# A state-space input stage fully unrolled over three chunks in flight, with the convolution accumulated in PSUM, and the y of the scan taken one state later

## The chip, the core and the metric

The kernel runs on one core of one Trainium2 chip. The metric is the time of one execution on the device in microseconds, as the median of several runs. The engines are TensorE (PE; its weight loads are PEld), VectorE (DVE), ScalarE (ACT), GpSimd (POOL) and SyncE (SP), which issues the DMAs.

## The reference

Four layers follow each other on a (4, 1024, 256) input: a Mamba layer, a top-2 mixture of experts, an attention, and a mixture in which the experts choose their tokens. The change lies in the first one only, whose mathematics is this (channels d_inner = 512, states 16, 4 taps):

```python
xz = hidden_states @ in_proj_w
x, z = jnp.split(xz, 2, axis=-1)
...
for k in range(D_CONV):
    acc = acc + conv_w[:, k] * xpad[:, k:k + seqlen, :]
x = jax.nn.silu(acc + conv_b)
x_dbl = x @ x_proj_w
dt_low, Bm, Cm = jnp.split(x_dbl, [DT_RANK, DT_RANK + D_STATE], axis=-1)
dt = jax.nn.softplus(dt_low @ dt_proj_w + dt_bias)
...
    dA = jnp.exp(dt_t[:, :, None] * A)
    dBu = dt_t[:, :, None] * B_t[:, None, :] * u_t[:, :, None]
    h = dA * h + dBu
    y_t = jnp.einsum('bdn,bn->bd', h, C_t)
...
y = jnp.swapaxes(y, 0, 1) + D_param * x
y = y * jax.nn.silu(z)
return y @ out_proj_w
```

## The kernel before

The layer runs as three blocks with a barrier between them: layernorm with a transpose, the input stage `mamba_front`, and the scan `mamba_scan`. All arithmetic here is float32; only the split B and C rows are bfloat16.

**Input stage.** The 4096 tokens are cut into 8 chunks of CH = 512. A chunk has MT = 4 blocks of 128 channels for x and 4 for z. For each of the 8 blocks TensorE multiplies with `w_in` into one of three PSUM banks (0, 1, 3; line 322). ScalarE copies the x blocks into `xpad` (369), VectorE runs the 4-tap convolution from `xpad` into `conv` in SBUF: one tensor_scalar (426) and three scalar_tensor_tensor (430) per block, with two blocks interleaved so that each instruction waits for the one before the last. ScalarE applies Silu to z (378) and to `conv` (381, giving `xc`, the u of the scan). TensorE multiplies `xc` with `w_x` (333) to 96 rows: 64 rows `dt_low`, which ScalarE copies (363), and 32 rows B and C, which VectorE copies (440) and splits into three bfloat16 parts (442 to 456). TensorE multiplies `dt_low` with `w_dt` (345) into the four PSUM banks 4 to 7.

The softplus is max(v, 0) + log(1 + e^-|v|), where the logarithm gets a correction for the rounding of its argument: VectorE takes the positive part `relu` (410), ScalarE |v| (388) and the exponential e (391), VectorE w = 1 + e (446), ScalarE the logarithm `lw` (394), VectorE the correction (w - 1) - e (450), GpSimd adds `relu` to `lw` (474), VectorE subtracts the correction (463), which gives `dt`, and GpSimd multiplies dt by `xc` (479), which gives `du`. SyncE writes z, x, B and C, dt and du of the chunk to DRAM, 1 MB each but for the 64 KB of B and C.

Step q does the head of chunk q (in_proj, convolution, Silu) and the tail of chunk q - 1 (x_proj, dt_proj, softplus). Every engine walks the steps in its own written order; the steps 2 to 7 are three rounds of a hardware loop of two steps each. Buffers `xc` and `zs` are double; ScalarE waits ahead of its z blocks until GpSimd has finished `du` of two chunks before, which reads the `xc` that is to be overwritten: `act.wait_ge(soft_pool, SP * (q - 1))`.

**Scan.** A unit is one state s of one channel block m of one batch b, over the whole sequence of 1024: 256 units. For 12 of 16 states TensorE spreads a row of B over the partitions (624), VectorE multiplies it with `du` in PSUM (705); for the four states 3, 7, 11 and 15 GpSimd makes the product (775). ScalarE makes dA (687), VectorE runs the recurrence (717), GpSimd multiplies with C (788), and TensorE sums the 16 states of a group into banks 4 and 5 with an identity (634), three units late (`LAG = 3`). The finished sum of a group is read by VectorE in the next group: `take_y` (724) adds D * x, `gate_y` (734) multiplies with silu(z), and out_proj (646) follows a batch later, with its additions to the residual (739).

```python
if s == FIN and not first:
    take_y(*before)
scan(b, m, s, first)
```

`FIN` is LAG - 1 = 2 here: VectorE reads y ahead of the recurrence of state 2. TensorE's sum for state 0 of the new group waits for `y_read`, since it overwrites the banks.

## Time and profile before

| What | us |
|---|---|
| Median of 3 runs | 3065.36 (3064.15 to 3067.4) |
| The profiled execution | 3070.39, of it span 3068.4 |
| Layernorm and transpose | 0 to 36.2 |
| Input stage | 36.2 to 343.5 |
| Scan with its out_proj | 343.5 to 1235 |
| The three other layers | 1235 to 3068.4 |

In rows by stage the engines stand in the order PE, PEld, DVE, ACT, POOL. The profile gives, for each engine, busy time, single instructions with their start and length, and the idle time ahead of an instruction with the instruction that ended it. The granted clock of TensorE (PEclk) is 1.00 at 2.4 GHz and 0.50 at 1.2 GHz. A float32 matmul appears as two passes, each with its weight load. The four stages follow each other behind barriers, so a stage that ends earlier moves all that follows.

### The profile page before, as it was taken

How to read it: one execution, taken by the hardware profiler on the slowest of the kernel's cores; microseconds unless marked ns; L12 is line 12 of the kernel's file. 1: busy time of each engine (PE TensorE's matmuls, PEld its weight loads, DVE VectorE, ACT ScalarE, POOL GpSimd, SP SyncE). 2: the span in 40 equal slices, each digit the busy share in tenths (PEclk: the TensorE clock that was granted, in tenths of full speed). 3: DMA queues.
4: the chain of work that ended last, by engine and by line, in shares of the span. 5: the costliest groups of instructions: out<-in, count | busy, mean ns of one | idle time of the engine just before them, and what ended most of it. 6: DMA issues, size and time to landing. Idle time of an engine off the chain costs nothing. (4 is left out here: it accounts for less than half of the span.)

```text
span 3068.4 us, 36222 instructions
## 1 busy us (share of the span) xinstructions
PE 2399.6 (78%) x10411; PEld 1261.6 (41%) x10413; DVE 1995.2 (65%) x2898; ACT 1028.3 (34%) x1511; POOL 1265.6 (41%) x696
## 2 busy tenths in 40 slices
PE   6676377777777877389994669999999733999998
PEld 3222132333333333256773313444444321666666
DVE  6888899999999998643333787868686265121110
ACT  3554333333333332212222605646465420211111
POOL 0334688888888887046651320000000001233332
PEclk9877688988988999689996859999999855999999
DMA  3333612313214110644433331202020032232322
GB/s 109 132 119 111 223 52 96 124 42 115 90 41 147 59 41 14 215 105 65 65 60 77 103 39 29 42 18 40 18 39 2 4 110 77 59 72 62 82 60 30
DMA packets 141562, 228.91 MB, mean 75 GB/s; under 512 B 25536, under 2 KB 89600, under 8 KB 141120
## 3 DMA queue, kind: packets, MB, share of 16 engines
q1 hardware_dynamic: 115312, 191.23, 20.0%
q0 software_dynamic: 26112, 35.96, 7.3%
q8 instruction: 72, 1.18, 0.2%
q14 instruction: 66, 0.54, 0.1%
HBM read 149.81 MB, written 77.34 MB: 74 GB/s over the span
## 5 line engine op out<-in xcount | busy, mean ns | idle before, releaser
L788 POOL TENSOR_TENSOR scan_hC<-scan_h,scan_c_all 128x1024 f32<-128x1024 f32 x256 | 612.2, 2404 | 108.3 <-DVE scan_h L717 106.5
L634 PE MATMUL banks<-scan_hC,all_ident 128*128 128x512 f32 x1024 | 534.1, 656 | 1.7 <-POOL scan_hC L788 1.7
L717 DVE TENSOR_TENSOR_SCAN scan_h<-scan_dA,banks 128x1024 f32<-128x1024 f32 x192 | 438.9, 2286 | 17.6 <-ACT scan_dA L687 1.6
L1760 ACT ACTIVATE attn_pt<-banks 128x256 f32<-128x256 f32 (+7 forms) x512 | 314.3, 651 | 333.8 <-PE banks L1688 329.6
L687 ACT ACTIVATE scan_dA<-scan_dt,mamba_a_neg 128x1024 f32<-128x1024 f32 x192 | 220.7, 1150 | 416.1 <-DVE scan_h L717 412.6
L1781 DVE TENSOR_REDUCE attn_m_lo<-banks 128x1 f32<-128x512 f32 (+3 forms) x512 | 288.1, 587 | 79.3 <-PE banks L1636 53.6
L624 PE MATMUL banks<-mamba_bc_parts,scan_pick 96*128 (+1 forms) x384 | 137.0, 444 | 242.6 <-DVE scan_h L717 206.9
L634 PEld LDWEIGHTS banks<-scan_hC,all_ident 128*128 128x128 f32 x1024 | 217.2, 212 | 206.6 <-issue 180.0
L1633 PE MATMUL banks<-attn_K,attn_Q 96*128 96x512 bf16 (+3 forms) x768 | 248.2, 357 | 44.9 <-DVE attn_mask L1773 27.4
L2250 DVE TENSOR_TENSOR ffn_y<-banks,ffn_gates 128x512 f32<-128x512 f32 x32 | 22.1, 692 | 358.6 <-PE banks L2149 351.8
L705 DVE TENSOR_TENSOR banks<-scan_du,banks 128x1024 f32<-128x1024 f32 x192 | 232.0, 1208 | 3.2 <-DMA scan_du<-scratch_du 3.2
L1686 PE MATMUL banks<-attn_Q,attn_K 99*128 99x512 bf16 (+3 forms) x768 | 209.3, 335 | 25.6 <-ACT attn_pt L1760 12.0
L2149 PE MATMUL banks<-ffn_w,ffn_hT 128*128 128x256 f32 x1024 | 228.6, 380 | 0.0
L2133 PE MATMUL banks<-ffn_xgT,ffn_w 128*128 128x512 f32 x512 | 228.5, 599 | 0.0
L2086 POOL DMA_INDIRECT out<-ffn_y,ffn_ids x64 | 101.0, 1578 | 296.7 <-DVE ffn_y L2250 287.0
L1616 POOL COPY attn_V<-attn_v_all 128x256 f32 x12 | 4.8, 402 | 505.2 <-PE banks L1705 505.2
L2149 PEld LDWEIGHTS banks<-ffn_w,ffn_hT 128*128 128x128 f32 x1024 | 191.9, 190 | 28.5 <-issue 4.3
L624 PEld LDWEIGHTS banks<-mamba_bc_parts,scan_pick 96*128 96x128 bf16 x384 | 31.6, 106 | 401.3 <-DVE scan_h L717 306.3
L2075 POOL DMA_INDIRECT ffn_xg<-scratch_xn_rows,ffn_ids x64 | 62.8, 981 | 307.1 <-DVE ffn_ids L2235 284.3
L1705 PE MATMUL banks<-attn_pt,attn_V 128*32 128x512 f32 (+3 forms) x1536 | 162.9, 499 | 1.7 <-issue 0.7
L775 POOL TENSOR_TENSOR scan_dBu<-scan_du,scan_b_all 128x1024 f32<-128x1024 f32 x64 | 150.9, 2358 | 11.6 <-DMA scan_b_all<-scratch_bc 11.6
L1633 PEld LDWEIGHTS banks<-attn_K,attn_Q 96*128 96x128 bf16 x768 | 76.6, 101 | 190.4 <-DVE attn_m_lo L1781 65.4
(267 smaller groups left out, 3814.8 us busy)
## 6 DMA issues: line engine op xcount, KB each, us to landing
scan_c_all<-scratch_bc SPq DMA_DIRECT2D x64, 512.0 KB, 4.8
ffn_w<-in_e_w SPq DMA_DIRECT2D x16, 1024.0 KB
attn_Q<-scratch_q SPq DMA_DIRECT2D x96, 128.0 KB
scratch_z<-front_zs SPq DMA_DIRECT2D x8, 1024.0 KB
scratch_x<-front_xc SPq DMA_DIRECT2D x8, 1024.0 KB
scratch_dt<-front_dt SPq DMA_DIRECT2D x8, 1024.0 KB
scratch_du<-front_du SPq DMA_DIRECT2D x8, 1024.0 KB
scan_dt<-scratch_dt SPq DMA_DIRECT2D x16, 512.0 KB, 6.2
```

The source lines that it names most:

```text
L624: mm = pe.matmul(PS[:, (s % 2) * HALVES + i, :], pick[:, s, :], bc_parts[:, bass.ds(b * SEQ + i * BANK, BANK)], start=True, stop=True)
L634: mm = pe.matmul(PS[:, YB + i, :], ident[:, :], hC[:, s % NHC, i * BANK:(i + 1) * BANK], start=s == 0, stop=s == NST - 1, skip_group_check ...
L687: act.activation(to, dt[:, m % 2, :], ACT.Exp, scale=a_neg[:, m, s:s + 1]).then_inc(dA_done, 1)
L705: dve.tensor_tensor(pair_of(s), du[:, m % 2, :], pair_of(s), ALU.mult).then_inc(dve_bu, 1)
L717: dve.tensor_tensor_scan(h[:, s % 2, :], decay, drive, 0.0, ALU.mult, ALU.add).then_inc(scanned, 1)
L788: pool.tensor_tensor(hC[:, s % NHC, :], h[:, s % 2, :], c_all[:, s, :], ALU.mult).then_inc(hC_done, 1)
L1633: mm = pe.matmul(PS[:, bank, at:at + width], Q[0:KR, mkv, j, tile * P:(tile + 1) * P], K[0:KR, mkv, k0:k0 + width], start=True, stop=not d ...
L1686: mm = pe.matmul(PS[:, b0 + i, 0:wd], K[:, kv, kb * P:(kb + 1) * P], Q[:, kv, j, kb * P + at:kb * P + at + wd], start=True, stop=i > 0, sk ...
L1760: act.activation(pt[:, kb % 2, j, 0:width], PS[:, SB_ + (j % 2) * 2:SB_ + (j % 2) * 2 + 2, :].rearrange("p a n -> p (a n)")[:, 0:width], A ...
L1781: op = dve.tensor_reduce(dst, PS[:, bank, at:at + width], AX, ALU.max)
L2133: mm = pe.matmul(PS[:, HB + (hp % 2) * 2 + i, :], w1[:, s, k, (2 * hp + i) * P:(2 * hp + i + 1) * P], xgT[:, pr, k, :], start=k == 0, stop ...
L2149: mm = pe.matmul(PS[:, YB + z, hf * DM:(hf + 1) * DM], hT[:, pr, c, j * P:(j + 1) * P], w2[:, s, c, :], start=c == 0, stop=c == HC - 1, sk ...
```

## The change

`mamba_front` is written anew, and in `mamba_scan` one number changes.

- Three chunks are in flight in place of two. Step q (of 10, all unrolled, no loop) does the head of chunk q, the projections and |v| of chunk q - 1 (`mid`), and the exponential, logarithm and the rest of the softplus of chunk q - 2 (`tail`). `xc` has four buffers.
- The convolution of a block accumulates in PSUM bank 3 and only its last tap writes `conv` in SBUF. With one bank for it the four blocks run one after the other, each instruction waiting for the one just before it.
- The positive part is not kept: `relu` and e are added in the PSUM bank of v, `less` = (w - 1) - (relu + e) is made from it by VectorE, and GpSimd's `lw - less` is dt. The second pass of VectorE over dt (463) is gone.
- The rows of `w_x` are reordered, so that B and C come first, and ScalarE copies all 96 rows at once into `xd`; a row of ones in `xd` and a row of `w_dt` carry dt_bias. Three memsets of 512 columns prepare `xd` and `w_dt`, and TensorE and ScalarE wait for them (`made`) ahead of their first instruction.
- The x, x_proj and z results rotate through the banks 0 to 2; each waits until the result three places before it was read.
- `FIN = LAG`: y is taken ahead of state 3, behind the recurrence of state 2.

In the diff below, removed lines that the code above shows already are left out.

```diff
-    w_dt = n.sb("w_dt", [RANK, DI])
+    w_dt = n.sb("w_dt", [XD + 1, DI])
...
+                               (w_x[:, :, 0:NBC], g["w_x"][:, RANK:XD].rearrange("(m p) n -> p m n", p=P)),
+                               (w_x[:, :, NBC:XD], g["w_x"][:, 0:RANK].rearrange("(m p) n -> p m n", p=P)),
+                               (w_dt[NBC:XD, :], g["w_dt"]),
+                               (w_dt[XD:XD + 1, :], g["dt_bias"].rearrange("(o d) -> o d", o=1)),
...
+        XS = 4
+        xc = n.sb("xc", [P, XS, MT, CH])
+        xd = n.sb("xd", [XD + 1, 2, CH])
+        less = n.sb("less", [P, MT, CH])
...
+        NIN, CBANK, DTBANK = 3, 3, 4
...
+        STEPS = range(NCH + 2)
+        PLACES = []
+        for q in range(NCH + 1):
+            PLACES += [("x", q, m) for m in range(MT) if head(q)]
+            PLACES += [("xd", q - 1, 0)] if mid(q) else []
+            PLACES += [("z", q, m) for m in range(MT) if head(q)]
+        def bank_of(kind, q, m):
+            return PLACES.index((kind, q, m)) % NIN
...
+            for q in STEPS:
+                if tail(q):
+                    c = q - 2
+                    sp.wait_ge(dt_done, MT * (c + 1))
+                    sp.dma_start(chunk_of("dt", c), lw[:, :, :]).then_inc(out_dt, 16)
+                    sp.wait_ge(du_done, MT * (c + 1))
+                    sp.dma_start(chunk_of("du", c), du[:, :, :]).then_inc(out_du, 16)
+                if mid(q):
+                    c = q - 1
+                    sp.wait_ge(xd_copied, c + 1)
+                    sp.dma_start(dram["bc"][:, c * CH:(c + 1) * CH], xd[0:NBC, c % 2, :]).then_inc(out_bc[c % 2], 16)
+                if head(q):
+                    sp.wait_ge(silu_x, MT * (q + 1))
+                    sp.dma_start(chunk_of("x", q), xc[:, q % XS, :, :]).then_inc(out_x[q % XS], 16)
+                    sp.dma_start(chunk_of("z", q), zs[:, q % 2, :, :]).then_inc(out_z[q % 2], 16)
...
+            def dt_proj(c):
+                pe.wait_ge(xd_copied, c + 1)
+                for m in range(MT):
+                    if c:
+                        pe.wait_ge(less_done, MT * (c - 1) + m + 1)
+                    pe.matmul(PS[:, DTBANK + m, :], w_dt[:, m * P:(m + 1) * P], xd[:, c % 2, :],
+                              start=True, stop=True).then_inc(dt_psum, 1)
+            for q in STEPS:
+                if head(q):
                     for m in range(MT):
+                        in_proj("x", q, m)
+                if mid(q):
+                    x_proj(q - 1)
+                if head(q):
+                    for m in range(2):
+                        in_proj("z", q, m)
+                if mid(q):
+                    dt_proj(q - 1)
+                if head(q):
+                    for m in range(2, MT):
+                        in_proj("z", q, m)
...
+            for q in STEPS:
+                if tail(q):
+                    c = q - 2
+                    act.wait_ge(dt_abs, MT * (c + 1))
+                    act.activation(u[:, :, :], u[:, :, :], ACT.Exp, scale=-1.0).then_inc(exp_done, 1)
+                if head(q):
+                    for m in range(2):
+                        copy_x(q, m)
+                if tail(q):
+                    c = q - 2
+                    act.wait_ge(w_done, c + 1)
                     for m in range(MT):
+                        act.activation(lw[:, m, :], w[:, m, :], ACT.Ln).then_inc(ln_done, 1)
+                if head(q):
+                    for m in range(2, MT):
+                        copy_x(q, m)
+                if mid(q):
+                    c = q - 1
+                    act.wait_ge(xd_psum, c + 1)
...
+                    act.activation(xd[0:XD, c % 2, :], PS[0:XD, bank_of("xd", c, 0), :], ACT.Copy).then_inc(xd_copied, 1)
+                if head(q):
+                    for m in range(2):
+                        silu_z(q, m)
+                    for m in range(2):
+                        silu_conv(q, m)
+                if mid(q):
+                    c = q - 1
                     for m in range(MT):
+                        act.wait_ge(dt_psum, MT * c + m + 1)
+                        act.activation(u[:, m, :], PS[:, DTBANK + m, :], ACT.Abs).then_inc(dt_abs, 1)
+                if head(q):
+                    for m in range(2, MT):
+                        silu_z(q, m)
+                    for m in range(2, MT):
+                        silu_conv(q, m)
...
-            dve.memset(xpad[:, :, 0:NTAP - 1], 0.0).then_inc(pad_zero, 1)
+            dve.memset(xpad[:, :, 0:NTAP - 1], 0.0).then_inc(made, 1)
+            for s in range(2):
+                dve.memset(xd[XD:XD + 1, s, :], 1.0).then_inc(made, 1)
+            dve.memset(w_dt[0:NBC, :], 0.0).then_inc(made, 1)
...
+            def convolve(q, m):
+                h = q % HB
+                acc = PS[:, CBANK, :]
+                for tap in range(NTAP):
+                    src = xpad[:, m, h * CH + tap:h * CH + tap + CH]
+                    if tap == 0:
+                        dve.wait_ge(x_copied, MT * q + m + 1)
+                        if q or m:
+                            dve.wait_ge(conv_step, NTAP * (MT * q + m))
+                        dve.tensor_scalar(acc, src, taps[:, m, 0:1], cbias[:, m:m + 1],
+                                          ALU.mult, ALU.add).then_inc(conv_step, 1)
+                    else:
+                        dve.wait_ge(conv_step, NTAP * (MT * q + m) + tap)
+                        if tap == NTAP - 1 and q:
+                            dve.wait_ge(silu_x, MT * (q - 1) + m + 1)
+                        dve.scalar_tensor_tensor(out=conv[:, m, :] if tap == NTAP - 1 else acc, in0=src,
+                                                 scalar=taps[:, m, tap:tap + 1], in1=acc, op0=ALU.mult,
+                                                 op1=ALU.add).then_inc(conv_step, 1)
+            def softplus_terms(c):
+                dve.wait_ge(exp_done, c + 1)
+                if c:
+                    dve.wait_ge(ln_done, MT * c)
+                    dve.wait_ge(less_done, MT * c)
+                dve.tensor_scalar(w[:, :, :], u[:, :, :], 1.0, None, ALU.add).then_inc(w_done, 1)
+                for m in range(MT):
+                    dve.scalar_tensor_tensor(out=PS[:, DTBANK + m, :], in0=PS[:, DTBANK + m, :], scalar=0.0,
+                                             in1=u[:, m, :], op0=ALU.max, op1=ALU.add).then_inc(relu_e, 1)
+                dve.wait_ge(w_done, c + 1)
+                for m in range(MT):
+                    if c:
+                        dve.wait_ge(dt_done, MT * (c - 1) + m + 1)
+                    dve.wait_ge(relu_e, MT * c + m + 1)
+                    dve.scalar_tensor_tensor(out=less[:, m, :], in0=w[:, m, :], scalar=1.0, in1=PS[:, DTBANK + m, :],
+                                             op0=ALU.subtract, op1=ALU.subtract).then_inc(less_done, 1)
...
+            for q in STEPS:
+                if tail(q):
+                    softplus_terms(q - 2)
+                if head(q):
                     for m in range(MT):
+                        convolve(q, m)
+                if mid(q):
+                    split_bc(q - 1)
...
+            for c in range(NCH):
+                for m in range(MT):
+                    pool.wait_ge(ln_done, MT * c + m + 1)
+                    pool.wait_ge(less_done, MT * c + m + 1)
+                    pool.tensor_tensor(lw[:, m, :], lw[:, m, :], less[:, m, :], ALU.subtract).then_inc(dt_done, 1)
+                if c:
+                    pool.wait_ge(out_du, 16 * c)
+                pool.wait_ge(silu_x, MT * (c + 1))
+                for m in range(MT):
+                    pool.wait_ge(dt_done, MT * c + m + 1)
+                    pool.tensor_tensor(du[:, m, :], lw[:, m, :], xc[:, c % XS, m, :], ALU.mult).then_inc(du_done, 1)
...
-        FIN = LAG - 1
+        FIN = LAG
```

On VectorE one step of the input stage now reads as follows, here step 1 of before with the tail of chunk 0 (`conv_step`, `soft_act` and the like are the semaphores waited for; a DVE row with x6 is six instructions of one form).

```order
L426 TENSOR_SCALAR front_conv<-front_xpad,mamba_taps,mamba_cbias 128x512 [waits front_silu_x,front_x_copied] x2
L430 SCALAR_TENSOR_TENSOR front_conv<-front_xpad,mamba_taps,front_conv 128x512 [waits front_conv_step] x6
L410 TENSOR_SCALAR front_relu<-banks,mamba_dtbias 128x512 [waits front_dt_psum] x4
L426 TENSOR_SCALAR front_conv<-front_xpad,mamba_taps,mamba_cbias 128x512 [waits front_silu_x,front_x_copied] x2
L430 SCALAR_TENSOR_TENSOR front_conv<-front_xpad,mamba_taps,front_conv 128x512 [waits front_conv_step] x6
L440 COPY front_bc<-banks 32x512 [waits front_xd_psum]
L442 CAST mamba_bc_parts<-front_bc 32x512 [waits front_xd_bc]
L444 TENSOR_TENSOR front_bc_rest<-front_bc,mamba_bc_parts 32x512 [waits front_bc_dve]
L446 TENSOR_SCALAR front_w<-front_u 128x2048 [waits front_soft_act]
L450 SCALAR_TENSOR_TENSOR front_w<-front_w,front_u 128x512 [waits front_soft_act] x4
```

Behind these rows before has three more of the split and the four of line 463. The same engine in step 3 of the changed kernel, from the softplus of chunk 1 to the first convolved block of chunk 3:

```order
L479 TENSOR_SCALAR front_w<-front_u 128x2048 [waits front_less_done,front_ln_done,front_exp_done]
L481 SCALAR_TENSOR_TENSOR banks<-banks,front_u 128x512 x4
L488 SCALAR_TENSOR_TENSOR front_less<-front_w,banks 128x512 [waits front_relu_e,front_dt_done,front_w_done]
L488 SCALAR_TENSOR_TENSOR front_less<-front_w,banks 128x512 [waits front_relu_e,front_dt_done] x3
L463 TENSOR_SCALAR banks<-front_xpad,mamba_taps,mamba_cbias 128x512 [waits front_conv_step,front_x_copied]
L469 SCALAR_TENSOR_TENSOR banks<-front_xpad,mamba_taps,banks 128x512 [waits front_conv_step] x2
L469 SCALAR_TENSOR_TENSOR front_conv<-front_xpad,mamba_taps,banks 128x512 [waits front_silu_x,front_conv_step]
```

The softplus stands ahead of the convolution and no longer waits for ScalarE between its instructions; the convolved block is a chain of four. ScalarE's order in step 3 of the changed kernel, the step in which the exponential comes first:

```order
L404 ACT_TABLE_LOAD
L404 ACTIVATE front_u<-front_u 128x2048 [waits front_dt_abs]
L384 ACTIVATE front_xpad<-banks 128x512 [waits front_conv_step,front_in_psum] x2
L415 ACT_TABLE_LOAD [waits front_w_done,front_du_done]
L415 ACTIVATE front_lw<-front_w 128x512 [waits front_out_dt]
L415 ACTIVATE front_lw<-front_w 128x512 x3
L384 ACTIVATE front_xpad<-banks 128x512 [waits front_conv_step,front_in_psum] x2
L426 ACTIVATE front_xd<-banks 96x512 [waits front_bc_dve,front_out_bc0,front_dt_psum,front_xd_psum]
L398 ACT_TABLE_LOAD [waits front_out_z1]
L398 ACTIVATE front_zs<-banks 128x512 [waits front_in_psum] x2
L392 ACTIVATE front_xc<-front_conv 128x512 [waits front_conv_step] x2
L439 ACTIVATE front_u<-banks 128x512 [waits front_dt_psum,front_relu_e,front_w_done]
```

The exponential stood behind |v| of its own step before; now a whole head lies between the two, and the wait for GpSimd's `du` has moved from the z blocks to the logarithm. In the scan, VectorE's rows around the take of y, before:

```order
L705 TENSOR_TENSOR banks<-scan_du,banks 128x1024 [waits scan_b_psum]
L724 SCALAR_TENSOR_TENSOR scan_xc<-scan_xc,mamba_d_par,banks 128x1024 [waits scan_xz_in,scan_summed]
L717 SCALAR_TENSOR_TENSOR scan_h<-scan_dA,banks 128x1024 [waits scan_hC_done,scan_dve_bu,scan_dA_done]
L717 SCALAR_TENSOR_TENSOR scan_h<-banks,scan_dBu 128x1024 [waits scan_hC_done,scan_pool_bu,scan_dA_done]
```

and now:

```order
L750 TENSOR_TENSOR banks<-scan_du,banks 128x1024 [waits scan_b_psum]
L762 SCALAR_TENSOR_TENSOR scan_h<-scan_dA,banks 128x1024 [waits scan_hC_done,scan_dve_bu,scan_dA_done]
L769 SCALAR_TENSOR_TENSOR scan_xc<-scan_xc,mamba_d_par,banks 128x1024 [waits scan_xz_in,scan_summed]
L762 SCALAR_TENSOR_TENSOR scan_h<-banks,scan_dBu 128x1024 [waits scan_hC_done,scan_pool_bu,scan_dA_done]
```

The take has moved behind one recurrence; the lines 762 and 769 are the former 717 and 724.

## Rows read from the trace of the kernel before

**Rows 1.** Stages: length, busy us (count) per engine, granted clock, DMA share, GB/s

```profile
36.20:343.50 307.30, 200.14 (x384) 76.74 (x384) 238.60 (x281) 138.71 (x200) 104.51 (x64) 0.78 0.31 113
343.50:1235.00 891.50, 678.42 (x1664) 298.97 (x1664) 844.19 (x514) 293.76 (x258) 757.67 (x320) 0.89 0.25 85
```

**Rows 2.** Who waited for whom, input stage; us in total, times, longest

```profile
ACT L378 <- POOL front_du L479: 58.7, 6, 10.3
...
PE banks L333 <- DVE front_bc L440: 43.0, 6, 7.7
...
DVE front_w L446 <- ACT front_u L391: 35.3, 8, 7.8
```

**Rows 3.** VectorE timeline, one step; start, us, engine, line, operation [idle before]

```profile
192.41 1.23 DVE L446 TENSOR_SCALAR front_w<-front_u 128x2048 f32<-128x2048 f32 x1 [4.24 <-ACT front_u L391]
...
202.78 4.64 DVE L463 TENSOR_TENSOR front_dt<-front_lw,front_w 128x512 f32<-128x512 f32 x4
...
210.15 4.05 DVE L430 SCALAR_TENSOR_TENSOR front_conv<-front_xpad,mamba_taps,front_conv 128x512 f32<-128x512 f32 x6
...
228.08 1.23 DVE L446 TENSOR_SCALAR front_w<-front_u 128x2048 f32<-128x2048 f32 x1 [4.24 <-ACT front_u L391]
```

**Rows 4.** Single lines of VectorE: count, min/median/max ns, first and last start

```profile
L426 DVE TENSOR_SCALAR front_conv<-front_xpad,mamba_taps,mamba_cbias x32: 537/546/1485, 39.1 to 288.7; 128x512 f32<-128x512 f32 x32
...
L410 DVE TENSOR_SCALAR front_relu<-banks,mamba_dtbias x32: 741/744/751, 68.2 to 316.4; 128x512 f32<-128x512 f32 x32
...
L450 DVE SCALAR_TENSOR_TENSOR front_w<-front_w,front_u x32: 692/1751/1768, 87.5 to 327.1; 128x512 f32<-128x512 f32 x32
...
L705 DVE TENSOR_TENSOR banks<-scan_du,banks x192: 1205/1206/1229, 348.5 to 1207.6; 128x1024 f32<-128x1024 f32 x192
...
L724 DVE SCALAR_TENSOR_TENSOR scan_xc<-scan_xc,mamba_d_par,banks x16: 1270/1279/1282, 407.4 to 1218.0; 128x1024 f32<-128x1024 f32 x16
```

**Rows 5.** Group of one line, 36 to 350 us: busy us, mean ns | idle before

```profile
L381 ACT ACTIVATE front_xc<-front_conv 128x512 f32<-128x512 f32 x32 | 18.7, 623 | 24.1 <-DVE front_conv L430 23.9
```

**Rows 6.** Timeline, end of the input stage

```profile
303.43 5.80 PE L345 MATMUL banks<-front_dt_low,mamba_w_dt 64*128 64x512 f32 x8 [3.75 <-ACT front_dt_low L363]
...
317.92 1.28 ACT L391 ACT_TABLE_LOAD   x1
...
317.93 0.41 DVE L442 CAST mamba_bc_parts<-front_bc 32x512 bf16<-32x512 f32 x1
318.38 0.68 DVE L444 TENSOR_TENSOR front_bc_rest<-front_bc,mamba_bc_parts 32x512 f32<-32x512 f32 x1
319.21 1.91 ACT L391 ACTIVATE front_u<-front_u 128x2048 f32<-128x2048 f32 x1
...
321.15 1.23 DVE L446 TENSOR_SCALAR front_w<-front_u 128x2048 f32<-128x2048 f32 x1 [2.10 <-ACT front_u L391]
...
338.38 0.37 SPq L298 DMA_DIRECT2D scratch_du<-front_du  x1
343.48 0.35 SPq L586 DMA_DIRECT2D scan_dt<-scratch_dt  x1
```

**Rows 7.** Timeline of the first steps, and a later gap of TensorE

```profile
36.25 13.97 PE L322 MATMUL banks<-mamba_xnT,mamba_w_in 128*128 128x512 f32 x32 [0.94 <-PEq L70]
36.29 0.07 DVE L400 MEMSET front_xpad<- 128x12 f32 x1 [1.75 <-PEq L70]
...
52.98 6.71 PE L333 MATMUL banks<-front_xc,mamba_w_x 128*96 128x512 f32 x8 [2.76 <-ACT front_xc L381]
...
105.00 3.78 PE L322 MATMUL banks<-mamba_xnT,mamba_w_in 128*128 x4 [3.90 <-ACT front_zs L378]
```

**Rows 8.** Scan stage: waits, groups by line, and the last y

```profile
DVE scan_xc L724 <- PE banks L634: 12.1, 8, 4.6
...
L788 POOL TENSOR_TENSOR scan_hC<-scan_h,scan_c_all 128x1024 f32<-128x1024 f32 x256 | 612.2, 2404 | 108.3 <-DVE scan_h L717 106.5
...
1217.99 1.28 DVE L724 SCALAR_TENSOR_TENSOR scan_xc<-scan_xc,mamba_d_par,banks 128x1024 f32<-128x1024 f32 x1 [4.61 <-PE banks L634]
```

275 lines of the change are left out of this document (88 added, 187 removed).

## The prediction

> **What bounds the kernel now.** I read the stages first. The change touches two of them, the input stage of 307.3 us and the scan of 891.5 us [rows 1]. In the input stage no engine is busy throughout: VectorE 238.6 us, TensorE 200.1, ScalarE 138.7, GpSimd 104.5, and TensorE's mean granted clock is 0.78. So the stage is bound by a loop through several engines. The waits show it [rows 2]: ScalarE waits 58.7 us in all for GpSimd's `du` ahead of its z blocks, TensorE 43.0 us for VectorE's copy of B and C, VectorE 35.3 us for the exponential. The timeline gives the period: line 446 starts at 192.41 and at 228.08, so a step takes 35.67 us [rows 3]. VectorE is idle for 4.24 us of it and else works, a good part of that slowed: line 450 takes 1751 ns in the median and 692 at best, line 426 up to 1485 against 546 [rows 4]. Where GpSimd runs beside VectorE, instructions with two inputs in SBUF or with one input and the output in SBUF take two to three times as long. Instructions with one side in PSUM don't: line 705 stays within 1205 to 1229 ns and line 724 within 1270 to 1282 over the whole scan, where GpSimd is busy for 757.7 of 891.5 us [rows 1, 4]. In the scan VectorE is the bound, with 844.2 of 891.5 us busy [rows 1].
>
> **The loop of the changed input stage.** ScalarE starts a step with the exponential, whose table load stands behind the last Silu of the step before; that Silu needs the last convolved block; VectorE convolves behind the softplus, and that needs the exponential. One turn, priced from rows:
> - w (446): 1.23 [rows 3].
> - Four additions in PSUM (481) and four `less` (488): one SBUF and one PSUM input each, so undisturbed, as lines 705 and 724. Six independent ones of line 430 take 4.05, that is 0.675 each [rows 3]: 8 x 0.675 = 5.40.
> - The convolution: 16 instructions, each waiting for the one before. The length is that of line 410 or 430, 0.744 [rows 4]; for the first tap, from SBUF into PSUM, which has no row, I bound it by 0.546 (426) and 0.744 (410) and take the PSUM row, as the nearer one. A dependent instruction starts 0.04 behind its predecessor's end (317.93 + 0.41 to 318.38) [rows 6]. 16 x 0.785 = 12.56. Before, the interleaved pairs paid 0.675 a tap, so this edit alone costs 16 x 0.11 = 1.8.
> - Silu 0.62 [rows 5], table load 1.28, exponential 1.91 [rows 6], and some 0.15 of hand-overs.
>
> The sum is 23.15 us a turn. The five instructions of the split lie in VectorE's wait for the exponential (0.62 + 1.28 + 1.91 = 3.81 us, against 0.41, 0.68, 0.41, 0.41 and 0.68 for them by lines 442 and 444 [rows 6], GpSimd being done by then), with about 1 us to spare. GpSimd has 8 instructions; at 2404 ns for 1024 columns undisturbed [rows 8] they take 8 x 1.2 = 9.6. ScalarE has three tables and 22 instructions, about 18 us. Four DMAs of 1 MB a turn need 178 GB/s; the last `du` is issued at 338.38 and the next block starts at 343.48 [rows 6], so 1 MB lands within 5.1 us, four in 20.4, with spare buffers for x.
>
> TensorE is the near second. 32 passes take 13.97 us at the full clock [rows 7], 0.437 each; a chunk has 32 for x and z, 8 for x_proj and 8 for dt_proj, 48 passes or 21.0 us. So it will idle for some 2 us a turn, at the fourth x block, whose bank is freed only by the first copy behind the exponential. Such a gap costs: behind 2.76 us idle eight passes took 6.71, behind 3.90 us four took 3.78, both about the 1.2 GHz level [rows 7]. If half speed lasts 3.5 to 6.5 us, 1.7 to 3.3 us are lost; walking ScalarE's order with the latter (x_proj ends 9.1 behind the exponential, dt_proj 16.0, z 19.4, then two Silus of z, two of x and the exponential) gives a turn of 24.8. That leaves no gap, so the next turn is warm again. I take 23.9, between 23.15 and 24.8.
>
> **Ends of the stage.** Start: three memsets of 512 columns now stand ahead of the first matmul. The row has 12 columns in 0.07 [rows 7]; bounds are 3 x 0.07 and 3 x 0.744, taken 3 x 0.6 = 1.8, the nearest row of 512 columns being 0.546. TensorE then goes through the first 80 passes (two heads, x_proj and dt_proj of chunk 0), 80 x 0.437 = 35.0, to 73.1. A last z and two Silus of x, the table and the exponential add 5.3, and half a gap's loss of clock 0.9: first exponential done at 79. Six turns follow: 79 + 6 x 23.9 = 222.4. Drain: x_proj of the last chunk runs ahead of this point and its copy ends 5.4 behind it (behind the logarithms); dt_proj 5.8 [rows 6] to 11.2; |v| 1.0; table and exponential 3.2 to 15.4; w, four additions and the first `less` 4.7 to 20.1; GpSimd 8 x 1.2 to 29.8; the DMA 5.1 [rows 6] to 35. The scan would start at 257.4, not 343.5: **86.1 us less**. For comparison, before used 8.6 of its turns for the same work.
>
> **Scan.** VectorE waits for TensorE ahead of line 724 eight times, 12.1 us in all [rows 8]. One wait, 4.61, is the last y, behind the loop, and stays. The other seven, 7.5 us, lie at the take in the next group, and none exceeds 1.4. With one recurrence (2.28) between, the sum is done. Late next would be TensorE's sum for state 0, which waits for the take: GpSimd needs it only four units on, some 8 us after state 2, and take plus sum at half speed are 1.28 + 3.5. So **7.5 us less**; bounds 0 and 9.
>
> **Sum.** 3068.4 - 86.1 - 7.5 = 2974.8 of span. The profiled execution is 2 us over its span and 5 us over the median; as a difference against the median, 3065.36 - 93.6 = 2971.8.
>
> **Two rules of the Trainium skill.** The table load is 1.28 us in the rows and the exponential follows at 319.21, at once. The Trainium skill, page "ScalarE: Activation LUTs", section "What ACT_TABLE_LOAD costs", gives about 2.66 us for each switch, with a drain. By it the turn would be 24.5 and the whole some 8 us slower, 2980; the rows are against it. Line 426 with both sides in SBUF takes 546 ns, line 410 out of PSUM 744. The Trainium skill, page "VectorE: DVE Perf Modes", section "Why PSUM operands drop a tier", says that a PSUM operand takes the doubled rate away in float32, which speaks against a first tap into PSUM: 0.2 us each, 4.8 us over six turns, which the sum holds already.
>
> **Rivals.**
> - *The convolution still collides with GpSimd.* Its source is in SBUF. For it: line 426 reads the same tile and went to 1485 [rows 4]. Against: lines 705 and 724 read SBUF too and never did. If only the first taps of three blocks suffer, 3 x 0.74 = 2.2 a turn, 13 in all: 2985. If all taps beside GpSimd's 10 us double, 7 a turn, 42 in all: 3014.
> - *TensorE becomes the bound at half speed (slower than before).* 48 passes at 0.86, the rate of 52.98, are 41.3 a turn. Six turns of 41.3, the start at 38 + 69 + 5 and the drain give about 395 for the scan's start, 51 later than before: 3109. It needs idle gaps in every turn and no recovery between; it beats the old kernel only below a turn of 38.6. Against it: a TensorE that is late has no gaps, and the clock came back within 7 us in each row.
> - *The wait for y moves and does not vanish.* The sum then holds for the input stage alone: 2979.
> - *DMA bound*: writes at no more than the 113 GB/s of the stage's mean [rows 1] would make a turn of 38; but that mean is of demand, and the landing above speaks for 206.
> - *The switch rule above*: 2980.
>
> **How the numbers follow.** Forecast, turn of 22.4 to 24.8 and the wait gone or moved: 0.78 (of it the moved wait 0.08). Light collision 0.08, heavy 0.06. Table drain 0.02. Half speed or DMA bound 0.03. Something outside these, on either side, 0.03. The likeliest case alone spans 2959 (turn 22.4, -9; ends -4) to 2988 (turn 24.8, +5.4; ends +3; no gain in the scan, +7.5). To reach the light collision I go to 2992. A measurement of this kernel tells 0.2%, 6 us. Faster 0.96, within 0.2% 0.01, slower 0.03.
>
> **What would show it.** Line 479 (w) every 23 to 25 us, with some 1 us of idle ahead; the lines 463 and 469 at 0.74 to 0.75 with GpSimd beside them; 38.1 for the first matmul; scan from 257; line 769 without idle but for the last. The prediction is wrong if PSUM accumulation has a latency between dependent instructions that no row shows, if table loads wait, or if TensorE's clock stays low.

## The result, and the profile after

The changed kernel takes 2976.14 us in the median of 4 runs (2972.46 to 2978.59), the kernel before 3065.97 beside it: ratio 0.9706, with a 95% interval of 0.9691 to 0.972, 89.8 us less. The forecast was 2971.8, 4.3 below. Its profiled execution has a span of 2973.1 us against 3068.4.

The stages, as in [rows 1]: length, busy us (count) per engine, granted clock, DMA share, GB/s. The third row is all that follows the scan.

```profile
36.20:251.50 215.30, 176.94 (x384) 73.52 (x384) 173.00 (x244) 136.33 (x200) 80.36 (x64) 0.90 0.44 161
251.50:1140.90 889.40, 676.18 (x1664) 294.40 (x1664) 844.97 (x514) 293.57 (x258) 757.96 (x320) 0.90 0.25 85
1140.90:2973.10 1832.20, 1506.34 (x8299) 873.80 (x8300) 890.82 (x2032) 579.40 (x1023) 402.81 (x308) 0.89 0.28 62
```

The input stage is 92.0 us shorter (215.3 against 307.3), the scan only 2.1 (889.4 against 891.5), the unchanged rest 1.2. The input stage moves 161 GB/s in place of 113. VectorE's busy time in the input stage fell from 238.6 to 173.0 us, and TensorE's granted clock rose from 0.78 to 0.90.

VectorE's timeline over one turn, from one start of line 479 to the next, the counterpart of [rows 3]:

```profile
148.57 1.23 DVE L479 TENSOR_SCALAR front_w<-front_u 128x2048 f32<-128x2048 f32 x1 [1.27 <-ACT front_u L404]
149.71 2.49 DVE L481 SCALAR_TENSOR_TENSOR banks<-banks,front_u 128x512 f32<-128x512 f32 x4
152.11 2.47 DVE L488 SCALAR_TENSOR_TENSOR front_less<-front_w,banks 128x512 f32<-128x512 f32 x4
154.49 0.81 DVE L463 TENSOR_SCALAR banks<-front_xpad,mamba_taps,mamba_cbias 128x512 f32<-128x512 f32 x1
155.34 1.55 DVE L469 SCALAR_TENSOR_TENSOR banks<-front_xpad,mamba_taps,banks 128x512 f32<-128x512 f32 x2
156.92 0.75 DVE L469 SCALAR_TENSOR_TENSOR front_conv<-front_xpad,mamba_taps,banks 128x512 f32<-128x512 f32 x1
...
167.45 0.41 DVE L495 CAST mamba_bc_parts<-front_xd 32x512 bf16<-32x512 f32 x1
...
171.46 1.23 DVE L479 TENSOR_SCALAR front_w<-front_u 128x2048 f32<-128x2048 f32 x1 [1.27 <-ACT front_u L404]
```

A turn is 171.46 - 148.57, 22.89 us; seven starts of line 479 lie 22.88 apart. The first stands at 79.92. The step of before took 35.67, and its rows between those of [rows 3] tell where VectorE spent it:

```profile
194.35 5.72 DVE L450 SCALAR_TENSOR_TENSOR front_w<-front_w,front_u 128x512 f32<-128x512 f32 x4 [0.71 <-ACT front_lw L394]
...
207.34 2.89 DVE L426 TENSOR_SCALAR front_conv<-front_xpad,mamba_taps,mamba_cbias 128x512 f32<-128x512 f32 x2
...
214.24 2.73 DVE L410 TENSOR_SCALAR front_relu<-banks,mamba_dtbias 128x512 f32<-128x512 f32 x4
...
221.88 0.68 DVE L440 COPY front_bc<-banks 32x512 f32<-32x512 f32 x1
```

Softplus and positive part, with three instructions of the split between them, took 14.93 (192.41 to 207.34) and 2.64 (214.24 to 216.88), 17.6 in all; now softplus takes 5.92 (148.57 to 154.49). The convolution took 11.9 and takes 12.96; the rest of the step, in which the exponential is waited for, took 6.2 and takes 4.0. So of the 12.8 us by which a turn is shorter, the softplus stretch has 11.6: fewer instructions, none of them slowed, and no split in its midst. The convolution itself became 1.1 longer.

GpSimd and TensorE in the same turn of the changed kernel:

```profile
152.93 4.96 POOL L520 TENSOR_TENSOR front_lw<-front_lw,front_less 128x512 f32<-128x512 f32 x4 [13.00 <-ACT front_lw L415]
157.84 4.96 POOL L526 TENSOR_TENSOR front_du<-front_lw,front_xc 128x512 f32<-128x512 f32 x4
```

```profile
149.08 1.98 PE L339 MATMUL banks<-mamba_xnT,mamba_w_in 128*128 128x512 f32 x4 [2.01 <-ACT front_xpad L384]
150.90 3.60 PE L347 MATMUL banks<-front_xc,mamba_w_x 128*96 128x512 f32 x8
...
171.96 3.53 PE L339 MATMUL banks<-mamba_xnT,mamba_w_in 128*128 128x512 f32 x4 [2.01 <-ACT front_xpad L384]
...
194.85 1.98 PE L339 MATMUL banks<-mamba_xnT,mamba_w_in 128*128 128x512 f32 x4 [0.32 <-ACT front_xpad L384]
```

GpSimd works from 152.93 to 162.80, so it runs beside three blocks of the convolution, and these take no longer for it: a block starts every 3.29 us, beside GpSimd or not. TensorE idles 2.01 us ahead of the fourth x block. In this turn the next passes run at the full clock (granted 1.00 from 147 to 155 us). Behind the same gap in the next turn they don't: the four passes at 171.96 take 3.53 us in place of 1.98, and the granted clock is 0.57 from 172 to 176, mostly the 1.2 GHz level. The turn stays at 22.88, since TensorE makes up for it out of its next gap, which is 0.32. The gap of 2.02 at 103.31 is followed by slow passes too.

In the scan the take of y (769) waits once only, for the last y (4.6 us, the first row of the waits below). But VectorE now stands still twice where its hardware loop jumps back (between the second block of a batch and the third):

```profile
576.35 1.21 DVE L750 TENSOR_TENSOR banks<-scan_du,banks 128x1024 f32<-128x1024 f32 x1
580.52 2.29 DVE L762 TENSOR_TENSOR_SCAN scan_h<-scan_dA,banks 128x1024 f32<-128x1024 f32 x1 [2.96 <-issue]
```

VectorE's waits, from 250 to 1250 us; total, times, longest (`issue` is a wait for nothing that the profile shows):

```profile
DVE scan_xc L769 <- PE banks L679: 4.6, 1, 4.6
...
DVE scan_h L762 <- issue: 3.0, 1, 3.0
DVE scan_h L762 <- POOL scan_hC L833: 2.2, 1, 2.2
```

The second stall is put down to GpSimd's product, but the recurrence at 798.42 needs only the product of two units before, which was done by then; both stand at the jump. The DMA view of the first, 570 to 585 us, has a row that the same place of the kernel before (664 to 679) has not:

```profile
q14 instruction: 2, 0.02, 0.3%
```

Two packets of 8 KB of code are fetched in this window, in which four loads of 512 KB run too.

### The profile page after: what moved, and what is told of

It is laid out like the page before. It is cut to its first block and busy times, and to the rows that moved or that the text cites. A ratio compares the mean times of both kernels' runs of the same rounds, so it can differ in the third digit from the quotient of the medians.

```text
span 2973.1 us, 35670 instructions
## 1 busy us (share of the span) xinstructions
PE 2371.3 (80%) x10411; PEld 1252.0 (42%) x10413; DVE 1932.7 (65%) x2861; ACT 1025.0 (34%) x1511; POOL 1241.3 (42%) x696
## 5 line engine op out<-in xcount | busy, mean ns | idle before, releaser
L669 PE MATMUL banks<-mamba_bc_parts,scan_pick 96*128 (+1 forms) x384 | 130.3, 425 | 222.8 <-DVE scan_h L762 197.9
L2295 DVE TENSOR_TENSOR ffn_y<-banks,ffn_gates 128x512 f32<-128x512 f32 x32 | 22.1, 692 | 359.1 <-PE banks L2194 352.4
L1731 PE MATMUL banks<-attn_Q,attn_K 99*128 99x512 bf16 (+3 forms) x768 | 208.9, 334 | 25.6 <-ACT attn_pt L1805 11.9
```

The source lines that it names most:

```text
L1731: mm = pe.matmul(PS[:, b0 + i, 0:wd], K[:, kv, kb * P:(kb + 1) * P], Q[:, kv, j, kb * P + at:kb * P + at + wd], start=True, stop=i > 0, sk ...
```

## The experiments

Time is the median of 4 or 5 runs. The kernel before took 3065.89 beside fin_only, front_only, conv_sbuf and conv_pair, 3068.03 beside pad42, pad80, pe_heavy and pe_light, and 3065.15 beside the rest, so across these groups a difference of 2 to 3 us says nothing. Beside the time stand readings of each trace: start of the first recurrence of the scan, and the time from there to the start of the last addition to X, which is the scan itself.

| Run | Time | First recurrence | Scan |
|---|---|---|---|
| before | 3065.97 | 349.82 | 884.88 |
| changed | 2976.14 | 257.85 | 882.60 |
| fin_only | 3052.88 | 348.45 | 876.19 |
| front_only | 2979.20 | 258.79 | 885.93 |
| front_pad | 2974.81 | 258.68 | 886.07 |
| pad42 | 2972.74 | 258.30 | 879.79 |
| pad80 | 2978.31 | 257.88 | 885.43 |
| conv_sbuf | 3005.24 | 283.56 | 883.79 |
| serial | 3024.30 | 309.29 | 884.21 |
| conv_pair | 2969.66 | 252.93 | 883.27 |
| pe_heavy | 2989.73 | 274.41 | 882.88 |
| pe_light | 2967.76 | 252.09 | 885.54 |
| no_made | 2970.28 | 254.50 | 882.59 |
| best | 2955.83 | 245.34 | 878.23 |

What follows the scan, whose source none of them touches, takes from 1826.8 to 1834.0 us in these traces (span less the last addition's start). So for a few us the readings of the two stages say more than the medians.

### The scan: the moved take, and the jump

**fin_only**, the kernel before with

```diff
-        FIN = LAG - 1
+        FIN = LAG
```

> The kernel before with one edit of the change alone: y is taken one unit later in the scan (FIN = LAG). By the prediction the seven waits ahead of the take vanish and nothing comes in their place: 7.5 us faster than before, 3058. Rival 1: the take's place itself makes VectorE stand at the loop's jump back, 2.96 and 2.16 us in the trace of the changed kernel: then only 2.3 us faster, 3063, and the stalls are in this run too. Rival 2: those stalls come from the unrolled input stage ahead of the scan; then this run is 7.5 us faster and shows none.

Measured: 3052.88, ratio 0.9957 (0.9944 to 0.9971), 13.0 us less. The scan itself is 8.69 us shorter, where 7.5 was foretold; the rest of the difference between the two traces lies ahead of the scan (1.4) and behind it (2.4), where the edit changes nothing. The waits for y are gone but for the last, and no stall stands at the jump:

```profile
DVE scan_xc L724 <- PE banks L634: 4.6, 1, 4.6
```

From the end of the last recurrence ahead of the jump to the start of the next are 1.24 us here, as in the kernel before (4.08 and 3.28 in the changed one).

**front_only**, the changed kernel with the edit undone.

> The changed kernel with the scan's edit undone (FIN = LAG - 1), so the input stage alone. The scan should start where it does in the changed kernel, at 251.5 us, 92 us earlier than before. If the moved take brings 7.5 us and the stalls at the jump back come from the unrolled stage, this run is 7.5 us slower than the changed kernel (2983.6) and shows stalls of 2 to 3 us at the jump. If the moved take brings the stalls with it, this run is 2.3 us slower (2978.5) and has no stall there.

Measured: 2979.20, 3.1 us above the changed kernel; its waits:

```profile
DVE scan_xc L769 <- PE banks L679: 10.8, 6, 4.6
DVE scan_h L762 <- issue: 5.6, 2, 2.9
```

So the take without the unrolled stage has no stalls, and the unrolled stage without the take has both. They come with the input stage. The size foretold for that case (7.5 us slower) was missed; the scan is 3.33 us longer. The waits for y are 6.2 us here beside the last y, where before had 7.5, so a part of them may be hidden under the stalls; most of the difference between 3.33 and 8.69 stays open.

**pad42** and **pad80** put tiny memsets behind VectorE's last instruction of the input stage:

```diff
+            for i in range(42):
+                dve.memset(pad[:, i:i + 1], 0.0)
```

> The changed kernel with 42 tiny memsets (one column each) at the end of VectorE's program of the input stage, where VectorE then waits 12.9 us for the stage's end. In the compiled program VectorE's loop of the scan (354 instructions of 64 bytes) starts at instruction 508 in the kernel before and at 594 in the changed one; with the 42 it starts at 636, which is 508 plus 128, the same place within 8 KB. The trace shows two instruction packets of 8 KB at each jump back of the changed kernel and none in the kernel before. Theory: whether VectorE refetches code at the jump hangs on where the loop lies; then the stalls of 2.96 and 2.16 us vanish, the windows of the jumps show no instruction packet, and the kernel takes 5 us less than the changed one, 2971. Rival: the length of the unrolled stage itself or another engine's code is the cause: no change, 2976.

> The same with 80 memsets: the loop starts at 674, 38 instructions further. Theory: the place within 8 KB matters and not that something is put in; this place (34 of 128, where 124 was free of stalls and 82 was not) need not be a good one. If it is bad, stalls as in the changed kernel and 2976; if any shift helps, 2971. Rival: as above, 2976 in both.

Measured: 2972.74 and 2978.31, in the same group of runs: 5.6 us between them, where the two stalls of the changed kernel are 5.1. With 42, VectorE goes through the same jump without a stop,

```profile
577.18 1.21 DVE L753 TENSOR_TENSOR banks<-scan_du,banks 128x1024 f32<-128x1024 f32 x1
578.51 2.29 DVE L765 TENSOR_TENSOR_SCAN scan_h<-scan_dA,banks 128x1024 f32<-128x1024 f32 x1
```

and the windows of both jumps have no instruction packet. With 80, both have two again, and the stalls are back:

```profile
DVE scan_h L765 <- issue: 3.0, 1, 3.0
...
DVE scan_h L765 <- POOL scan_hC L836: 1.8, 1, 1.8
```

So it is the place of the loop in VectorE's code that decides. Free of stalls were starts at 508 and 636, both 124 above a multiple of 128 instructions (8 KB); stalled were 594 and 674. The loop has 354 instructions of 64 bytes, 22.1 KB. What rule stands behind the four places is not shown. One that would fit: the loop is kept while it touches three blocks of 8 KB (24 KB) and fetched again in part when it touches four, with a start of the blocks that no run shows. The other runs fit, though where the loop starts in most of them is not on record: both stalls, of 1.8 to 3.3 us, stand in conv_sbuf, serial, conv_pair, pe_heavy, pe_light and no_made, none of them padded, and neither in front_pad and best, which are padded so that the loop starts at 636. The Trainium skill, page "Runtime: NRT & Kernel Launch", section "Instruction fetch mechanics", says that a taken branch whose target isn't in the current window of two pages forces a fetch before execution goes on, and that a page is 16 KiB. The stall with its packets agrees. The page size doesn't fit as simply: if the loop were kept whenever it lies within two such pages, no start of the code would make 508 and 636 free and 594 and 674 stalled.

**front_pad**, the 42 memsets with the take where it was.

> The changed kernel with the scan's edit undone (FIN = LAG - 1) and the 42 tiny memsets, so that the scan's loop lies where the kernel before has it. Theory: with the stalls at the jump out of the way the moved take is worth what it is worth in the kernel before, 7.5 us by its waits (12.5 between the two profiled spans there): against the run with 42 memsets and the moved take (2972.7) this one is 7 to 9 us slower, 2980 to 2982. Rival: the moved take is worth only the 3 us that the pair without memsets shows (2979.2 against 2976.1): 2975 to 2976.

Measured: 2974.81, 2.1 us above pad42; by the traces the scan is 6.28 us longer (886.07 against 879.79), with the waits for y back at 13.0 in 8. The two medians come from different groups of runs; each set against the kernel before beside it (90.3 and 95.3 us less), front_pad is 5.0 us slower, between the rival's 3 and the theory's 7 to 9. The scan in the trace is nearer to the theory. Between the two profiled executions the difference is mostly taken back behind the scan: 1828.2 us there against 1832.9. So the moved take is worth 6 to 9 us in the scan where the loop lies well (6.28 here, 8.69 in fin_only), 3.3 where it lies badly. What the rest of the kernel does with it stays open.

### The input stage: what bounds the turn

**conv_sbuf**, the changed kernel with

```diff
-                acc = PS[:, CBANK, :]
+                acc = conv[:, m, :]
```

The wait for the Silu that frees `conv` moves to the first tap, and the wait of a block for the one before it, which the single bank needed, falls away.

> The changed kernel with all four taps of a block in the SBUF tile conv in place of the PSUM bank: the third chunk without the convolution in PSUM. Theory: taps with both sides in SBUF take 0.69 us alone and 1.75 beside GpSimd (the quick and the median row of the softplus instruction of before); GpSimd works some 10 of the 22.9 us of a turn, which holds 5.7 slowed taps; 16 taps then take 17.5 in place of 13.1, the turn 27.3, the kernel some 27 us slower than the changed one (15 to 45), about 3003. Rival: the gain lies in the chunks' overlap alone and the loop has slack on VectorE: within 5 us of the changed kernel.

Measured: 3005.24, 29.1 us above the changed kernel; the turn is 27.27, foretold 27.3. Two blocks of one turn, the first beside GpSimd (which works from 139.04 to 151.06), then the last one, with GpSimd idle:

```profile
140.61 1.23 DVE L463 TENSOR_SCALAR front_conv<-front_xpad,mamba_taps,mamba_cbias 128x512 f32<-128x512 f32 x1
141.87 4.99 DVE L467 SCALAR_TENSOR_TENSOR front_conv<-front_xpad,mamba_taps,front_conv 128x512 f32<-128x512 f32 x3
...
155.14 0.54 DVE L463 TENSOR_SCALAR front_conv<-front_xpad,mamba_taps,mamba_cbias 128x512 f32<-128x512 f32 x1
155.71 2.33 DVE L467 SCALAR_TENSOR_TENSOR front_conv<-front_xpad,mamba_taps,front_conv 128x512 f32<-128x512 f32 x3
```

A block takes 6.2 us beside GpSimd and 2.82 alone; from PSUM it is 3.29 in either place. So the bank costs 0.47 us a block where GpSimd is idle and saves 2.9 where it works. GpSimd is slowed as well: its eight instructions take 12.0 us here and 9.9 in the changed kernel. Of the 0.47 the first tap has 0.28 (0.85 from its start to the next in PSUM, 0.57 in SBUF) and the hand-over to the next block, which waits for the one bank, 0.19; the taps between cost the same in both. The Trainium skill, page "VectorE: DVE Perf Modes", section "Why PSUM operands drop a tier", says that with any PSUM operand float32 runs at the single rate. The trace agrees for the first tap: 0.81 us into PSUM, 0.54 into SBUF.

**serial** makes VectorE wait for GpSimd ahead of the convolution:

```diff
                 if head(q):
+                    if q >= 2:
+                        dve.wait_ge(du_done, MT * (q - 1))
```

> The changed kernel with one more wait: VectorE begins the convolution of a chunk only when GpSimd is through with its eight instructions. Theory: the convolution in PSUM runs beside GpSimd at no loss, and this is what the change lives on. In the trace it starts 6.1 us behind line 479's start and GpSimd ends 14.2 behind it, so the turn grows by 8.1 us to 31.0; six turns: 49 us slower than the changed kernel, 3025. Rival: the overlap is worth little since something else bounds the turn: under 20 us.

Measured: 3024.30, 48.2 us above the changed kernel (49 foretold); the turn is 31.21, 8.33 longer, and 8.26 of it are VectorE's new wait:

```profile
157.43 0.81 DVE L463 TENSOR_SCALAR banks<-front_xpad,mamba_taps,mamba_cbias 128x512 f32<-128x512 f32 x1 [8.26 <-POOL front_du L528]
158.28 1.55 DVE L469 SCALAR_TENSOR_TENSOR banks<-front_xpad,mamba_taps,banks 128x512 f32<-128x512 f32 x2
```

The taps are as long with GpSimd idle as beside it, to the hundredth. In the changed kernel all of them, beside GpSimd or not, lie within 8 ns by line (count, then min/median/max):

```profile
L463 DVE TENSOR_SCALAR banks<-front_xpad,mamba_taps,mamba_cbias x32: 809/814/817, 42.9 to 210.1; 128x512 f32<-128x512 f32 x32
L469 DVE SCALAR_TENSOR_TENSOR banks<-front_xpad,mamba_taps,banks x64: 754/756/757, 43.8 to 211.8; 128x512 f32<-128x512 f32 x64
```

So the rival of a collision is ruled out, and without the overlap of convolution and GpSimd the changed kernel would lose 48 of its 90 us.

**conv_pair** takes the taps of the blocks 0 and 1 in turns, the second in bank 7; dt_proj's last block waits for them.

```diff
+                for tap in range(NTAP):
+                    for m in range(2):
+                        tap_of(q, m, tap, PS[:, (CBANK, DTBANK + 3)[m], :], base if m == 0 else 0,
+                               base + 2 * (tap - 1) + m + 1)
```

> The changed kernel with the taps of its first two blocks taken in turns, the second block in PSUM bank 7, which is free between the softplus and the next dt_proj; so 8 of 16 taps don't wait for the one just before them. Theory: the chain costs 0.82 us a tap where independent instructions of this kind are issued every 0.62 to 0.68, and VectorE's work is the loop: turn 1.1 to 1.6 us shorter, 21.3 to 21.8 (TensorE's 21.0 is the floor), 7 to 10 us off the kernel, 2966 to 2969. Rival: the loop is bound elsewhere (TensorE with a lower clock, ScalarE), then no change within 2 us.

Measured: 2969.66, 6.5 us less than the changed kernel. The turn is 21.81; the eight taps take 5.39 us (129.10 to 134.49) where two blocks in a chain take 6.58:

```profile
129.10 1.53 DVE L463 TENSOR_SCALAR banks<-front_xpad,mamba_taps,mamba_cbias 128x512 f32<-128x512 f32 x2
130.54 2.72 DVE L469 SCALAR_TENSOR_TENSOR banks<-front_xpad,mamba_taps,banks 128x512 f32<-128x512 f32 x4
133.17 1.40 DVE L469 SCALAR_TENSOR_TENSOR front_conv<-front_xpad,mamba_taps,banks 128x512 f32<-128x512 f32 x2
134.49 0.81 DVE L463 TENSOR_SCALAR banks<-front_xpad,mamba_taps,mamba_cbias 128x512 f32<-128x512 f32 x1
```

A tap that waits for the one before costs 0.82 us, one that doesn't 0.67. The six turns bring 6.4 us, a little less than the 7 to 10 foretold. By the traces only 4.9 of it are left at the first recurrence, since the last two starts of w lie 16.32 us apart in place of 14.62.

**pe_heavy** and **pe_light** give TensorE eight passes more or fewer a chunk. The heavy one issues each matmul of dt_proj twice, as below; the light one leaves out the second half of the contraction for z, so its z is incomplete and its time serves as a reading only.

```diff
-                    pe.matmul(PS[:, DTBANK + m, :], w_dt[...], xd[...], start=True, stop=True).then_inc(dt_psum, 1)
+                    for twice in range(2):
+                        mm = pe.matmul(PS[:, DTBANK + m, :], w_dt[...], xd[...], start=True, stop=True)
+                    mm.then_inc(dt_psum, 1)
```

> The changed kernel with each matmul of dt_proj issued twice (the second overwrites the first with the same numbers): 8 more passes a chunk, 3.5 us of TensorE at the full clock. Theory (VectorE and ScalarE bound the turn, TensorE has 2.01 us to spare): the last z tile comes 3.5 us later, 19.9 behind the exponential; a Silu of z, two of x, the table and the exponential make a turn of 24.9 in place of 22.9; 12 us in six turns, 3.5 more at the start and about 3.5 in the drain: 19 us slower than the changed kernel (14 to 24), about 2995. Rival: TensorE is already on the loop; then 3.5 a turn, 28 us or more slower in all, 3004 or more.

> The changed kernel with only the first of the two slices of the contraction for the z tiles, so z is incomplete: 8 passes fewer a chunk, TensorE's gap ahead of the fourth x block grows from 2.0 to about 5.5 us a turn. Theory: the turn stays at 22.9 us; only the start gets shorter, by the 16 passes less ahead of the first exponential, 7 us: 2969. The granted clock tells whether a gap of 5.5 us brings the lower level where 2.0 did not; that would not lengthen the turn. Rival: TensorE is on the loop, then the turn falls to 21.5 or less and the kernel to 2960 or less.

Measured: 2989.73 and 2967.76. The heavy run is 13.6 us above the changed kernel, just under the 14 to 24 foretold (19); by the traces the first recurrence is 16.6 later. Its turn is 24.58, 1.70 longer for 3.5 us more work (24.9 foretold); the light one is 22.88, the same as the changed kernel's. So TensorE has some 1.7 us to spare a turn, and taking work from it brings the turn nothing; what the light run gains, 5.8 us by the traces, lies ahead of the first exponential. In the light run it idles 3.74 us and then runs slow:

```profile
143.30 3.78 PE L340 MATMUL banks<-mamba_xnT,mamba_w_in 128*128 128x512 f32 x4 [3.74 <-ACT front_xpad L385]
146.87 4.67 PE L348 MATMUL banks<-front_xc,mamba_w_x 128*96 128x512 f32 x8
...
166.18 3.61 PE L340 MATMUL banks<-mamba_xnT,mamba_w_in 128*128 128x512 f32 x4 [2.62 <-ACT front_xpad L385]
```

The granted clock is 0.50 from 144 to 148 us (the 1.2 GHz level) and 1.00 from 152. It costs the turn nothing.

**no_made** lets TensorE and ScalarE start without VectorE's memsets:

```diff
             loads.wait(pe)
-            pe.wait_ge(made, 4)
...
             def dt_proj(c):
+                if c == 0:
+                    pe.wait_ge(made, 4)
```

> The changed kernel with TensorE and ScalarE not waiting for VectorE's four memsets at the start of the input stage (TensorE waits for them ahead of the first dt_proj, VectorE ahead of the first convolution). Theory: the first matmul starts at 36.3 as in the kernel before and not at 38.73; the x copies start as early and the first exponential is done 2.0 to 2.4 us earlier; the kernel 2 us faster than the changed one, 2974. Rival: the start is bound by TensorE's clock after its gap or by the first copies (42.2 in the trace of the changed kernel), so nothing or under 0.5 us.

Measured: 2970.28, 5.9 us less, where 2 was foretold; by the trace the first recurrence is 3.35 earlier and the scan is equal, so 3.4 of it belong to the edit. The first matmul starts at 37.11, not at 36.3. The first rows of TensorE, here,

```profile
37.11 20.84 PE L338 MATMUL banks<-mamba_xnT,mamba_w_in 128*128 128x512 f32 x48 [0.94 <-PEq L70]
```

and in the changed kernel:

```profile
38.73 22.53 PE L339 MATMUL banks<-mamba_xnT,mamba_w_in 128*128 128x512 f32 x48 [3.02 <-DVE mamba_w_dt L451]
```

The memsets cost 1.62 us of start and, behind the gap of 3.02, another 1.69 of slow passes.

**best** puts together conv_pair, no_made, the fourth block in SBUF (`conv[:, m, :]` as its accumulator) and 58 memsets.

> All that the runs point to together: the first two blocks' taps in turns in two PSUM banks (6.5 us in its own run), the third in PSUM, the fourth in SBUF, where the run with all taps in SBUF shows 2.82 us a block against 3.29 when GpSimd is done (0.47 a turn, 3 us in all), no wait for the memsets (2), and 58 tiny memsets that put the scan's loop at 636 (3.4). Sum: 15 us faster than the changed kernel, 2961; the turn 21.3 us, and TensorE's 21.0 is its floor. Rival: the fourth block still meets GpSimd or TensorE's clock falls in the turns: turn 21.8 to 22.5, 2964 to 2970.

Measured: 2955.83, ratio 0.964 (0.9627 to 0.9653) to before: 20.3 us less than the changed kernel, 5 more than the sum foretold. The turn is 21.34 and the loop's stalls are gone. GpSimd ends at 154.97, before the fourth block begins:

```profile
155.23 0.54 DVE L467 TENSOR_SCALAR front_conv<-front_xpad,mamba_taps,mamba_cbias 128x512 f32<-128x512 f32 x1
155.81 2.33 DVE L473 SCALAR_TENSOR_TENSOR front_conv<-front_xpad,mamba_taps,front_conv 128x512 f32<-128x512 f32 x3
```

By the traces 12.5 us lie ahead of the scan and 4.4 in it. The rest is within what the part behind the scan varies by.

## Why the prediction was right, and where not

- **The loop.** Shown. It was named as ScalarE's exponential, VectorE's softplus and convolution, the last Silu and the table load. pe_light leaves the turn alone, serial adds its wait in full, conv_pair takes off what VectorE is quicker by (1.07 of 1.19 us). What the prediction did not say is where on VectorE the gain over before lies: mostly in the softplus stretch, 11.6 of 12.8 us a turn.
- **The sum of the turn, 23.15.** Measured 22.88, with two errors that nearly cancel. The eight independent instructions take 4.78 (149.71 to 154.49), not 5.40; the chain takes 12.96 (154.49 to 167.45), not 12.56, since the first tap is 0.81 and not 0.744 and a block starts 0.11 behind the last tap of the one before (157.67 to 157.78), while within a block the 0.04 holds. w is 1.14 to the next start, not 1.23, and from the last tap to the next w 4.01, not 3.96.
- **23.9 taken for TensorE's clock.** This step failed: it added 0.75 us a turn for the lower clock, and the measured turn has nothing of it. The gap ahead of the fourth x block is 2.01 us as forecast ("some 2 us a turn"), and behind it the lower clock did come in some turns (103.31, 171.96) and not in another (149.08). Even the alternation was foreseen: behind a slow stretch the next gap is 0.3 us and the next passes are quick. But a slow stretch lengthens the passes by about 1.7 us (four of them by 0.4 each), the lower end of the 1.7 to 3.3 of the forecast, and that is what TensorE has to spare: the gap shrinks from 2.01 to 0.32, and the turn stays at 22.88. With 3.74 us of idle and a longer slow stretch (pe_light) it stayed there too. What was wrong is the walk along ScalarE's order, which let the loss reach the exponential. The six turns together are 6.1 us shorter than taken, nearly all of the difference between -92.0 and the -86.1 of the forecast.
- **Ends.** First exponential forecast at 79, found at 79.9; the drain 35, found 34.3 (217.2 to 251.5). The memsets were priced at 1.8 and half a gap's clock at 0.9: no_made shows 3.35 for both, against 2.7.
- **GpSimd, split, DMA.** Eight instructions take 9.9 us (9.6), the split fits into the wait with 1.27 to spare (about 1). The stage moves 161 GB/s on average where the DMA rival had set a bound of 113: that rival falls. In the drain instructions with both sides in SBUF do meet GpSimd: the last w takes 2.09 us (at 231.84) in place of 1.23, and the five of the last split, which has no convolution ahead of it, 1.2 to 1.6 in place of 0.4 to 0.7.
- **Table load.** 1.28 us, and the exponential follows at once. The Trainium skill, page "ScalarE: Activation LUTs", section "What ACT_TABLE_LOAD costs", gives about 1.28 for the load and about 2.66 with a drain. The load agrees; the drain doesn't show in the changed kernel either: from the last Silu's end to the exponential's start are 1.3 us (145.32 to 146.63).
- **The rival at half speed.** Its limit, a turn of 38.6 below which it would still beat the old kernel, doesn't come out of its own terms: with its start of 112 and the drain of 35 it is 33 to 34. Nothing else hangs on it.
- **The scan, -7.5.** The step was: with one recurrence between, the sum is done and no wait is left. Right by itself (fin_only, -8.69 in the scan). Wrong in this kernel, -2.3, since the unrolled input stage moves the scan's loop to a place where VectorE refetches code at each jump, 2.96 + 2.16 = 5.1 us. The prediction had not looked at code at all. That the place of the code brings the stalls was shown by pad42 and pad80.
- **The total** came within 4.3 us by luck, since these two errors have opposite signs: 5.9 us too little in the input stage, 5.2 too much in the scan. Of the 95.2 us between the two profiled executions 5.4 aren't in the medians: that of before lies 4.4 above its median, that of after 0.9 below.

What stays open: the shares of the third chunk, of the bank and of the shorter softplus. conv_sbuf keeps the first and the last and undoes the bank (29 us), serial undoes the overlap of GpSimd and convolution (48 us), and these two can't be added, since the one is what makes the other free. No run keeps the new softplus with two chunks in flight, or the old one with three, so the 11.6 us a turn of that stretch can't be split between fewer instructions, the bank of v and the new order. A variant with the additions of line 481 in SBUF wasn't tried.

## What to carry to other kernels

Find the loop that passes through the engines and price it in VectorE's starts, not its mean lengths: a tap that waits for its predecessor costs 0.82 us, one that doesn't 0.67, and where a second bank is free the difference is to be had. Accumulate in PSUM what must run beside GpSimd, and in SBUF what runs when it is idle; here both were quicker for it. An idle gap of TensorE is room as well: a slow stretch that loses less than the gap holds costs the turn nothing. After unrolling anything, look again at the hardware loops behind it: here a stall at the jump, marked as issue or as a wait that had long been met, with instruction packets in the DMA view, went away with 42 small instructions in a place where the engine waits anyway, and came back with 80.

## What the runs showed of the hardware that was not expected

- A VectorE loop of 354 instructions lost some 3 and 2 us at its two jumps or nothing, by where its code lay (594 and 674 against 508 and 636).
- Instructions with one side in PSUM kept their length beside GpSimd to the hundredth of a microsecond (a block 3.29 us in either case), while taps with SBUF on both sides went from 0.78 to 1.66 us and GpSimd's own eight instructions from 9.9 to 12.0.
- The same gap of 2.01 us in front of the same passes of TensorE was followed by the full clock in one turn (four passes 1.98 us at 149.08) and by half of it in the next (3.53 us at 171.96, granted clock 0.57 from 172 to 176). Gaps of 0.94 us in conv_pair, one a turn, were never followed by slow passes; those of 2.62 to 4.15 in the turns of pe_light always were.
